# Node stage of a four-layer graph network: the first norm's scaled row moves from VectorE to ScalarE, its square sums the other way

## The reference, cut to what matters

```python
x1 = _layernorm(x + attention(...) + (x @ W_skip + b_skip))     # norm 1
x2 = _layernorm(x1 + conv_layers(x1, ...))                      # norm 2; without edges: x1 + b3
x3 = _layernorm(x2 + layer(layer(x2, W3_0), W3_1))              # norm 3; leaky slope 0.229
x4 = _layernorm(x3 + ...)                                       # norm 4
```

## Time and profile before

| what | value |
|---|---|
| median of three runs | 4943.14 us (4939.24 to 4952.62) |
| the profiled execution's own time | 4908.06 us |
| its span in the trace | 4906.3 us |
| busy over the whole span: PE, DVE, ACT, POOL | 60%, 59%, 38%, 42% |
| node stage, by the starts of its first and last square roots | 1751.4 to 2736.9 us |
| DVE busy between 1900 and 2000 us (edge steps) | 96.84 of 100 us |
| DVE, ACT busy between 2400 and 2500 us (node steps) | 90.47, 88.44 of 100 us |

### The profile page before, as it was taken

One profiled execution on the slowest core, in us unless ns is written; L12 is line 12 of the kernel. 1 busy time (PEld: TensorE's weight loads), 2 busy tenths in 40 slices (PEclk: granted clock), 3 DMA queues, 4 the chain that ended last, 5 costly groups with the idle time before them and its releaser, 6 DMA issues. The chain is left out here.

```text
span 4906.3 us, 57671 instructions
## 1 busy us (share of the span) xinstructions
PE 2951.7 (60%) x14568; PEld 2124.4 (43%) x14568; DVE 2894.7 (59%) x8821; ACT 1848.3 (38%) x5406; POOL 2040.4 (42%) x1978
## 2 busy tenths in 40 slices
PE   2156455544995767677777376575554554677532
PEld 0002222223663555556665255454343454676431
DVE  4277555543446879999999333343664333678633
ACT  0001122113772256678888333232232332663010
POOL 7712666655650000000000475775664555560276
PEclk9966676666997988889999667666555766878655
DMA  3301222236764954432222255565564555773221
GB/s 93 101 21 51 83 82 81 83 78 158 240 223 132 308 155 138 133 102 91 87 89 82 80 188 167 165 193 181 176 192 143 183 176 172 216 226 116 82 79 58
DMA packets 533038, 662.62 MB, mean 135 GB/s; under 512 B 99744, under 2 KB 301412, under 8 KB 532710
## 3 DMA queue, kind: packets, MB, share of 16 engines
q1 hardware_dynamic: 466854, 558.03, 36.6%
q0 software_dynamic: 65856, 100.90, 7.5%
HBM read 441.19 MB, written 246.24 MB: 140 GB/s over the span
## 5 line engine op out<-in xcount | busy, mean ns | idle before, releaser
L1669 POOL DMA_INDIRECT xg_c<-x1d_d,src_row x196 | 214.7, 1095 | 1375.3 <-DMA xg_c<-x1s_d 1318.4
L1669 POOL DMA_INDIRECT xg_c<-r_d,src_row x392 | 419.9, 1071 | 213.0 <-issue 117.2
L1688 DVE TENSOR_TENSOR_SCAN agg_t_c<-flags_c,agg_t_c,t_ps_c 128x512 f32<-128x512 bf16 x144 | 183.7, 1276 | 263.4 <-remote 232.9
L369 PE MATMUL c_ps<-hot_hi,hot_lo 128*128 128x391 bf16 x392 | 161.9, 518 | 253.5 <-DVE hot_hi L357 140.7
L530 POOL DMA_INDIRECT row<-table_d,node_i x196 | 199.5, 1018 | 233.2 <-DVEq L555 173.7
L2383 POOL DMA_INDIRECT out<-x_f,out_row x196 | 197.6, 1008 | 218.1 <-DVE x_f L2449 161.8
L544 POOL DMA_INDIRECT rows_d<-row,slot_i x196 | 195.9, 999 | 199.2 <-DVEq L607 147.0
L1669 POOL DMA_INDIRECT xg_c<-x2d_d,src_row x196 | 198.7, 1014 | 184.2 <-DMA xg_c<-x2s_d 127.5
L1669 POOL DMA_INDIRECT xg_c<-g1d_d,src_row x196 | 203.0, 1035 | 158.8 <-DMA xg_c<-g1s_d 102.1
L1688 DVE TENSOR_TENSOR_SCAN agg_t_c<-flags_c,agg_t_c,term_t_c 128x512 f32<-128x512 bf16 x96 | 123.1, 1282 | 247.1 <-remote 172.3
L626 PE MATMUL run_ps<-hot_hi,hot_lo 128*128 128x391 bf16 x196 | 80.0, 408 | 288.2 <-ACT run L650 195.5
(11 more groups left out here) (431 smaller groups left out, 9417.8 us busy)
## 6 DMA issues: line engine op xcount, KB each, us to landing
flags_c<-cont_d SPq DMA_DIRECT2D x245, 128.0 KB
xm<-rows_d SPq DMA_DIRECT2D x49, 512.0 KB
x_n<-in_x SPq DMA_DIRECT2D x98, 256.0 KB
out<-x_n SPq DMA_DIRECT2D x98, 256.0 KB
m_d<-m_c SPq DMA_DIRECT2D x98, 256.0 KB
r_d<-r_c SPq DMA_DIRECT2D x98, 256.0 KB
m_in_c<-m_d SPq DMA_DIRECT2D x98, 256.0 KB
e_c<-rows_d SPq DMA_DIRECT2D x98, 256.0 KB
```

The source lines that it names most:

```text
L369: mm = pe.matmul(c_ps[s][:, 0:HI], hot_lo[:, t % 8, s, :], hot_hi[:, t % 8, s, 0:HI], start=(t == 0), stop=(t == TILES - 1))
L1669: pool.indirect_dma_start(out=xg[:, s, k, :], out_offset=None, in_=table, in_offset=bass.IndirectOffsetOnAxis(ap=src_row[:, t:t + 1], axis=0),
L1688: dve.tensor_tensor_scan(agg_t[:, n % 2, :], flags[:, n % SL, :], terms, agg_t[:, (n - 1) % 2, G - 1:G] if n else 0.0, ALU.mult, ALU.add). ...
```

## The change

In the node stage x1 of group it-2 is now made in both kinds of step by ScalarE, as the last item of its step: four 128-wide ACTIVATEs of kind Copy, each reading its chunk of `nm_ps` and scaled by its column of `inv` (new signal `x1_made`, three x1 buffers). VectorE adds b3 one step later, as the first item of its step (y2 of group it-3, one 512-wide add in SBUF). The squares of the product become one 512-wide ACTIVATE on ScalarE without accumulation, and VectorE sums them with one `tensor_reduce` in the middle of its step (new signal `summed_1`). PE's wait for the product's bank is on `x1_made` instead of `y2_ready`. The reciprocals have a signal of their own (`recip_made`).

```diff
 dense_sp
                 g = it - 3
                 if 0 <= g < GROUPS:
-                    sp.wait_ge(y2_ready.sem, y2_ready.at(g + 1))
-                    sp.dma_start(rows_of(x1s_d, g), x1[:, g % 2, :, :]).then_inc(s_out[g % 2].sem, 16)
+                    sp.wait_ge(x1_made.sem, x1_made.at(g + 1))
+                    sp.dma_start(rows_of(x1s_d, g), x1[:, g % 3, :, :]).then_inc(s_out[g % 3].sem, 16)
 dense_pe (product of g = it - 1)
                     if g >= 2:
-                        pe.wait_ge(y2_ready.sem, y2_ready.at(g - 1))
+                        pe.wait_ge(x1_made.sem, x1_made.at(g - 1))
 dense_act (g = it - 1)
                     act.wait_ge(made_1.sem, made_1.at(g + 1))
-                    for k in range(K):
-                        made = act.activation(sq1[:, k, :], nm_ps[g % 2][:, chunk(k)], ACT.Square, accum_out=ss1[:, k:k + 1])
-                    made.then_inc(squared_1.sem, 1)
+                    if g >= 1:
+                        act.wait_ge(summed_1.sem, summed_1.at(g))
+                    act.activation(flat(sq1[:, :, :]), nm_ps[g % 2][:, :], ACT.Square).then_inc(squared_1.sem, 1)
...
 dense_act (last item)
+                g = it - 2
+                if 0 <= g < NG:
+                    act.wait_ge(recip_made.sem, recip_made.at(it))
+                    if g >= 3:
+                        act.wait_ge(y2_ready.sem, y2_ready.at(g - 2))
+                        if edge(g - 3):
+                            act.wait_ge(s_out[g % 3].sem, s_out[g % 3].at(g // 3))
+                    for k in range(K):
+                        made = act.activation(x1[:, g % 3, k, :], nm_ps[g % 2][:, chunk(k)], ACT.Copy, scale=inv[:, it % 2, 0, k:k + 1])
+                    made.then_inc(x1_made.sem, 1)
 dense_dve (first item)
+                g = it - 3
+                if 0 <= g < NG:
+                    if g >= 6:
+                        dve.wait_ge(squared_2.sem, squared_2.at(g - 5))
+                    dve.wait_ge(x1_made.sem, x1_made.at(g + 1))
+                    dve.tensor_tensor(y2[:, g % 6, :, :], x1[:, g % 3, :, :], b3_mid[:, :, :], ALU.add).then_inc(y2_ready.sem, 1)
...
-                    dve.reciprocal(inv[:, now, :, :], spread[:, was, :, :]).then_inc(own.one(), 1)
+                    dve.reciprocal(inv[:, now, :, :], spread[:, was, :, :]).then_inc(recip_made.sem, 1)
+                    dve.wait_ge(recip_made.sem, recip_made.at(it))
                     done()
-                g = it - 2
-                if 0 <= g < GROUPS:
-                    if g >= 2:
-                        dve.wait_ge(s_out[g % 2].sem, s_out[g % 2].at(g // 2))
-                    dve.tensor_tensor(x1[:, g % 2, :, :], nm_ps[g % 2][:, :].rearrange("p (k d) -> p k d", k=K),
-                                      inv[:, now, 0, :].unsqueeze(2).to_broadcast([P, K, D]), ALU.mult).then_inc(x1s_ready.sem, 1)
-                elif GROUPS <= g < NG:
-                    dve.wait_ge(squared_2.sem, squared_2.at(g - 5))
-                    for k in range(K):
-                        made = dve.scalar_tensor_tensor(y2[:, g % 6, k, :], nm_ps[g % 2][:, chunk(k)], inv[:, now, 0, k:k + 1], b3_mid[:, k, :], ALU.mult, ALU.add)
-                    made.then_inc(y2_ready.sem, 1)
...
-                g = it - 2
-                if 0 <= g < GROUPS:
-                    if g >= 6:
-                        dve.wait_ge(squared_2.sem, squared_2.at(g - 5))
-                    dve.wait_ge(x1s_ready.sem, x1s_ready.at(g + 1))
-                    dve.tensor_tensor(y2[:, g % 6, :, :], x1[:, g % 2, :, :], b3_mid[:, :, :], ALU.add).then_inc(y2_ready.sem, 1)
+                g = it - 1
+                if 0 <= g < NG:
+                    dve.wait_ge(squared_1.sem, squared_1.at(g + 1))
+                    dve.tensor_reduce(ss1[:, :], sq1[:, :, :], AX.X, ALU.add).then_inc(summed_1.sem, 1)
                 if 1 <= it < NG + 8:
                     done()
                     dve.sem_inc(inv_ready.sem, 1)
...
                 g = it - 1
                 if 0 <= g < NG:
-                    dve.wait_ge(squared_1.sem, squared_1.at(g + 1))
+                    dve.wait_ge(summed_1.sem, summed_1.at(g + 1))
                     dve.tensor_scalar(spread[:, now, 0, :], ss1[:, :], 1.0 / D, EPS, ALU.mult, ALU.add).then_inc(own.one(), 1)
```

More of the change, by code:

```diff
@@ L1321, in graph_kernel @@
             x_t = sb("x_t_n", [P, 2, G], F32, st)
-            x1 = sb("x1_n", [P, 2, K, D], F32, st)
+            x1 = sb("x1_n", [P, 3, K, D], F32, st)
             y2 = sb("y2_n", [P, 6, K, D], F32, st)
@@ L1348, in graph_kernel @@
             x4_out = [signal(f"x4_out{s}", 16) for s in range(3)]
-            s_out = [signal(f"s_out{s}", 16) for s in range(2)]
+            s_out = [signal(f"s_out{s}", 16) for s in range(3)]
             x2_out = [signal(f"x2_out{s}", 16) for s in range(2)]
@@ L1352, in graph_kernel @@
             turned_x, xt_ready = signal("turned_x"), signal("xt_ready")
-            made_1, squared_1, x1s_ready = signal("made_1"), signal("squared_1"), signal("x1s_ready")
+            made_1, squared_1, x1_made, recip_made = signal("made_1"), signal("squared_1"), signal("x1_made"), signal("recip_made")
             y2_ready, turned_y, yt_ready, squared_2 = signal("y2_ready"), signal("turned_y"), signal("yt_ready"), signal("squared_2")
             made_2, sloped_g, g1_ready, made_3, leaked, halved = (signal(s) for s in ("made_2", "sloped_g", "g1_ready", "made_3", "leaked", "halved"))
-            summed_2, added_u = signal("summed_2"), signal("added_u")
+            summed_1, summed_2, added_u = signal("summed_1"), signal("summed_2"), signal("added_u")
             spread_ok, rooted_n, inv_ready, normed = signal("spread_ok"), signal("rooted_n"), signal("inv_ready"), signal("normed")
@@ L1605, in _ @@
                         sp.wait_ge(x4_out[s].sem, x4_out[s].at(len(range(s, NN, 3))))
+                    for s in range(3):
+                        sp.wait_ge(s_out[s].sem, s_out[s].at(shares(s, 3)))
                     for s in range(2):
-                        sp.wait_ge(s_out[s].sem, s_out[s].at(len(range(s, GROUPS, 2))))
                         sp.wait_ge(x2_out[s].sem, x2_out[s].at(len(range(s, GROUPS, 2))))
@@ L1630, in graph_kernel @@
             retire([(s, NG) for s in (turned_x, xt_ready, made_1, squared_1, y2_ready, turned_y, yt_ready, squared_2, made_2, sloped_g,
-                                      g1_ready, made_3, leaked, halved, summed_2, added_u)])
-            retire([(setup, 1), (spread_ok, NG + 7), (rooted_n, NG + 7), (inv_ready, NG + 7), (normed, NN)])
-            retire([(s, GROUPS) for s in (x1s_ready, x2s_ready, turned_g, g1o_ready)])
+                                      g1_ready, made_3, leaked, halved, summed_1, summed_2, added_u, x1_made)])
+            retire([(setup, 1), (spread_ok, NG + 7), (rooted_n, NG + 7), (inv_ready, NG + 7), (recip_made, NG + 7), (normed, NN)])
+            retire([(s, GROUPS) for s in (x2s_ready, turned_g, g1o_ready)])
             retire([(x_in[s], len(range(s, NG, 6))) for s in range(6)] + [(x4_out[s], len(range(s, NN, 3))) for s in range(3)])
-            retire([(group[s], shares(s, 2)) for group in (s_out, x2_out, g1_out) for s in range(2)])
+            retire([(group[s], shares(s, 2)) for group in (x2_out, g1_out) for s in range(2)] + [(s_out[s], shares(s, 3)) for s in range(3)])
         SC, SM, SL = 7, 6, 8
```

## The result

The changed kernel takes 5393.97 us in the median of four runs, the kernel before 4947.88 us in four; the ratio is 1.0909 (95% interval 1.0871 to 1.0946), some 446 us more. The direction was as forecast (5220 us), the size was not: the time lies outside the range of 5085 to 5345 us, some 174 us above the forecast and near rival (b), 5368 us. The profiled execution's span is 5395.6 us against 4906.3. The node stage, by the starts of its first and last square roots (L1447), now runs from 1775.8 to 3199.7 us, 1423.9 us instead of 985.5. These 438 us are nearly all of it.

The account below looks back on a forecast made before the run. DVE's list was taken to bound the node step at 5.96 us; a 7.49 us PE-ACT loop plus 1.4 us lost clock made 8.9, +264 us, edge steps +13, so 4943 became 5220 us, range 5085 to 5345.

Parts of the forecast that it names:

- rival (b): Node-stage loop with TensorE at its lower clock level in every step: 10.2 us node steps, 5368 us; chance 0.13.
- The bound: Node stage before the change: DVE's list sets the node step of 5.96 us, while PE is early and waits.
- The work moved: Node step: DVE's work changes by -0.06 us to 5.88, ACT's by +0.67; both would need about 5.9 us.
- The loop through ScalarE's last instruction: Node step: PE waits for ACT's x1, ACT for PE's product, so they alternate; 7.49 us at the upper clock level.
- TensorE's clock on that loop: Node step: PE's lost clock is now paid in full, 1.4 us a step (ends 0 and 2.76), making 8.9 us.
- the ring: The alternation of PE and ACT through x1 in node steps, forecast at 7.49 us without clock loss.
- bias rows every 10.2 us: Forecast sign in the node-step profile: bias rows every 7.5 or 10.2 us would mean the clock's share was wrong.
- the clock term: The 1.4 us a node step that TensorE's lower clock level was forecast to add to 7.49 us.
- (a): Rival: node-stage loop with a clock no worse than in the node steps of before, +180 us, 5123 us; chance 0.18.
- Edge steps: Same loop in edge steps: 7.4 us plus 0.75 of lost clock, 8.15 us; +13 us for 45 steps.
- (c): Rival: no loop decides in the node stage, DVE still sets the step at 5.88 us; 4938 us, chance 0.07.
- (d): Rival: ScalarE's scaled copies far slower than 406 ns while DVE is active, +36 us, 5256 us; chance within the forecast's 0.62.

Follow-up runs that it names:

- e10: The kernel before with 4 constant products added in PE's idle time of each node step, nothing waiting for them; ratio 1.0002.
- e4: The kernel before with only the squares' part of the change: one 512-wide square on ScalarE, one reduction on VectorE; ratio 1.0108, 56 us over before.
- e5: The changed kernel with x1 made by ScalarE between the square of y2 and the slope, not last; ratio 1.0021, node step 5.95 us.
- e2: The changed kernel with 12 constant products added on PE in each node step's idle time; ratio 1.0394, node step 7.41 us.
- e11: The changed kernel with a fifth output row, into an unread buffer, made by ScalarE in each node step; 424 us over before, node step 10.24 us.
- e8: The changed kernel with three of the four output rows made by ScalarE in each node step; ratio 1.0889, node step 10.24 us.
- e12: The changed kernel with two of the four output rows made by ScalarE in each node step; 166 us over before, node step 7.31 us.
- e9: The changed kernel with constant products on PE, 12 in each node step and 8 in each edge step; 140 us over before, edge step 7.91 us.
- e7: The changed kernel with 4 constant products added on PE in each node step's idle time; ratio 1.0422, node step 7.97 us.
- e1: The changed kernel with x1 made by ScalarE right behind the leaked slope, before the output rows, not last; ratio 1.0193, node step 6.82 us.

## Why the prediction failed, by its own steps

- **The bound.** DVE's list set the step before, with PE's clock losses hidden. Right; e10 shows that the clock's losses were hidden (clock to 1.00, ratio 1.0002), and e4 that work added to DVE's list lengthens the step.
- **The work moved.** The sums for DVE (-0.06) and ACT (+0.67) imply node steps of about 5.9 without a loop; e5 has 5.95. Four copies took 1.12 us in the changed kernel, 1.20 was forecast. Right.
- **The loop through ScalarE's last instruction.** Forecast 7.49 us at the upper level; e2 measures 7.41. PE waits for ACT's x1 3.33 us a step (3.4 forecast), ACT waits at its square 2.7 us (over 1), DVE at its add 4.0 us (2 to 3). Right in place; the waits on ACT and DVE were under-sized with the clock.
- **TensorE's clock on that loop: the step that failed.** "So I take 1.4, between 0.95 and 1.54 and near the latter." It measured 2.83 a step (10.24 - 7.41). The missing 1.43 us in each of 90 steps, less the 0.08 by which the ring itself was shorter than forecast, are 121 us. The fault was in how I read the rows of before. There DVE sets the period, so a slow PE step eats its own idle time: behind every slow node step (PE's part 5.7 us, once 7.28) the next idle time was under 0.3 us, and the step after was at the upper level again. One such step, which ends at 2404.29 us and is followed by the idle time of 0.20 in the earlier trace rows:

```profile
2398.54 0.37 PE L1402 MATMUL nm_ps<-row_three,ones_b 3*128 3x512 bf16 x1 [1.86 <-DVE y_n L1538]
2398.84 1.59 PE L1404 MATMUL nm_ps<-w_first,x_t_n 128*128 128x128 f32 x8
...
2403.24 1.05 PE L1436 MATMUL nu_ps<-w_L_gnn_W,g_t_n 128*128 128x128 f32 x8
```

The 21 edge steps from which I took the 1.54 have the same flaw: each of them follows a PE part of 4.08 us, as only behind a fast step 2.92 us were left. No step of before follows both a slow burst and an idle time of more than 1.7 us, and in the loop every burst does. There the idle time is ScalarE's work and does not shrink when PE is slow, so after every burst the same 3.33 us follow. A constant idle time alone does not keep the clock down, though: with 3.71, 3.33 and 2.95 us of it (e11, changed, e8) all 84 steps are slow, but with 2.57 (e12) only 24 are, and the others recover. So it is shown that the loss was 2.83 and the clock's. That the missing recovery made it so much larger than 1.4 fits these rows, but no run varied it by itself. The warning was in the prediction: it named the steady 3.4 us as longer than any idle time that it had read, and then took a mean below the largest loss (2.76 in its edge rows; one node step of before lost 3.20). It also named bias rows every 10.2 us as the sign that the clock term was wrong, and this is the sign that came.
- **Rival (b)** had 10.24 us a step by the 6.84 us of the longest edge step in the earlier trace rows, plus 40 us for the edges: 5368 us. It is what happened in every node step, but I gave it 0.13, less than (a), although the rule beside it spoke for (b). The range, too, reached 0.84 of the way from the forecast to (b), and not half of it as the prediction says. That its sum gave exactly 10.24 is in part luck: it adds 6.84 and 3.40 us where 6.91 and 3.33 were measured, and e8 and e11 keep 10.24 with PE's part at 7.28 and 6.53. The Trainium skill's statement that stood beside it (TensorE: Matmul & The Clock Gate, "HAM oscillation — how this bites in real kernels") describes a kernel in which PE waits for a transfer behind each short burst, long enough that every burst starts throttled. The trace of the changed kernel agrees: bias rows of 0.58 and product groups of 2.08 us in every step. It is not so in every loop with a wait: 60 of 84 steps of e12 run at the upper level behind 2.57 us.
- **Edge steps.** Forecast 8.15 us by a loss of 0.75; measured 8.86, a mean loss of 1.93 in PE's part (6.01 - 4.08) behind 2.41 us of idle time. I had argued that 2.4 is less than 2.92 and so loses less. This leans on the same mean. A second error went the other way: the forecast put the loop without loss at 7.4 us, and it is 6.93, as the first edge steps show in which PE lost nothing:

```profile
1808.88 0.37 PE L1402 MATMUL nm_ps<-row_three,ones_b 3*128 3x512 bf16 x1 [2.41 <-ACT x_n L1506]
...
1815.81 0.37 PE L1402 MATMUL nm_ps<-row_three,ones_b 3*128 3x512 bf16 x1 [2.41 <-ACT x_n L1506]
```

6.93 and 1.93 make the 8.86. e9 takes this share away (edge step 7.91). The same edge code (changed, e2, e7, e8, e11, e12) gave 8.19 to 8.86 us in different traces, so the share of the edge steps is less firm, 15 to 45 us.
- **Rivals (c) and (d).** (c), no loop that decides, is excluded by e2 and the waits. (d), slower copies beside a busy VectorE, is excluded: the group of L1506 in the changed kernel has a mean of 376 ns, less than the 406 of L1486 in the earlier trace rows:

```profile
L1506 ACT ACTIVATE x_n<-nm_ps,inv_n 128x128 f32<-128x128 f32 x588 | 167.2, 376 | 0.0
```

The sum of what was measured: 90 node steps x (10.24 - 5.96) = 385 us and 45 edge steps x 1.0 = 45 us, 430 of the 446 us; the stage's own growth is 438. Of the 169 us by which the forecast growth of 277 was short, 121 are the node steps' and 32 the edge steps'; the other 16 are not traced.

## What to carry to other kernels

Before a bank's release is moved to another engine, walk the ring that the two engines' lists form, from one wait to the next until it closes: if engine A's first item waits for B and B's first item waits for A's last, they alternate, and the place of one instruction in a list (e5 against the change, 1.002 against 1.091) is worth more than all the work it moves. When such a ring contains TensorE, do not price its clock at a mean loss from a schedule whose idle time shrinks when PE is slow. Here the largest losses in the trace (2.76 us in an edge step, 3.20 in a node step) were about what the ring lost with 3.33 us of idle time (2.83), but too much for rings with less: 0.66 with 2.57 us (e12) and 0.92 with 1.82 us (e1). So take no loss and the largest as the ends of the range, and expect the upper part of it where the idle time is longer than any that was read. A run with constant matmuls in the idle time tells the clock's part from the ring's.

## What the runs showed of the hardware

- A step held at a fixed length while TensorE's clock took up the difference: with ScalarE's part at 2.95, 3.33 or 3.71 us the period was 10.24 in each case, PE's part being 7.28, 6.91 and 6.53. Shaving 0.39 us off the critical engine gained nothing, and adding 0.39 cost nothing in the step; 0.38 us further down (2.57) the mean fell by 2.9 us at once.
- 0.9 us of useless matmuls in each step (e7) gave back 2.3 us of 10.24, and 2.7 us of them (e2) 2.83, with PE's own work at full speed in all 84 steps.
- A long PE part is not always a slow clock. In the edge steps of e5 it is 5.48 us in the mean, but in 22 of 37 steps nothing runs low, and the length is a wait for y2 of up to 0.8 us:

```profile
1960.10 0.66 PE L1422 MATMUL ny_ps<-ident,y_n 128*128 128x128 f32 x4 [0.81 <-DVE y_n L1520]
```

In the other 15 the clock did cost PE time, and the step is 7.92 us all the same, as it is in e9 at a granted clock of 1.00 (7.91): a low clock that nothing waits for costs nothing.
